# The prologue of a signature, attention and mixture-of-experts kernel: VectorE makes the first tile's levels, the norms come from Gram matrices

## The reference

```
x: 64 sequences x 64 steps x 7 channels; t is prepended: 8 channels
dx = x[:, 1:] - x[:, :-1]
levels 1 to 4 of the running path signature (8, 64, 512, 4096 values):
    e_k = outer(e_(k-1), dx) / k;  level_k += e_k + sum outer(level_i, e_(k-1-i))
h = concat(levels) @ W.T + b                                   # 4680 -> 128
h = h + attention(layernorm(h))    # 8 heads of 64, within a sequence, a token not to itself
h = h + moe(layernorm(h))          # 8 experts of 512, top 1, and a shared gelu expert

attention's weights are spectrally normed (one power iteration), for W = w_qkv and w_out:
    v = W @ u;  v = v / |v|;  u2 = W.T @ v;  u2 = u2 / |u2|
    sig = v @ W @ u2;  W / sig * sigma
```

## Time and profile before

| | |
|---|---|
| median of 3 runs | 715.73 us (715.45 to 715.82) |
| the profiled execution | 715.07 us, its span 713.1 us |
| TensorE busy over the span | 664.4 us, 93% |
| VectorE, GpSimd, ScalarE | 436.7, 334.1, 297.4 us |
| mean granted TensorE clock | 0.977 |
| prologue, up to TensorE's first product of iteration 0 | 54.10 us, TensorE busy 37.23 |
| iteration 0 | 14.33 us |

### The profile page before, as it was taken

How to read it: one execution, slowest core, us unless ns; L and a number is a source line. 1 busy time by engine, 2 the same in 40 slices (tenths; PEclk the granted TensorE clock), 3 DMA queues, 4 the chain that set the end, 5 groups by cost and what they waited for, 6 DMA issues and landing times.

```text
span 713.1 us, 13737 instructions
## 1 busy us (share of the span) xinstructions
PE 664.4 (93%) x3976; PEld 512.9 (72%) x3977; DVE 436.7 (61%) x1085; ACT 297.4 (42%) x701; POOL 334.1 (47%) x344
## 2 busy tenths in 40 slices
PE   4789999999999999999999999998879769999993
PEld 1567777777778777877777777876769737777772
DVE  6676776767766776767676776765374125445441
ACT  3314444454435444454435444443746124434440
POOL 5765453454435453455445443541027704544553
PEclk9799999999999999999999999999899979999998
DMA  8915221112211211112111211121244222323230
GB/s 329 171 64 203 49 47 33 37 34 61 63 37 33 58 37 37 33 44 52 33 37 33 63 33 37 33 56 41 66 173 136 75 56 40 42 39 41 38 41 5
DMA packets 40847, 45.28 MB, mean 63 GB/s; under 512 B 6272, under 2 KB 29184, under 8 KB 40448
## 3 DMA queue, kind: packets, MB, share of 16 engines
q1 hardware_dynamic: 34192, 40.86, 21.5%
q0 software_dynamic: 6640, 4.22, 4.3%
HBM read 17.30 MB, written 11.44 MB: 40 GB/s over the span
## 4 chain that ended last, share of the span: by engine, by line
PE 79%; POOL 8%; DVE 5%; issue 5%; DMA 1%; ACT 1%; SPq 0%; POOLq 0%; DVEq 0%
PE bank L1112 69%; POOL sorted_rows L523 4%; PE bank L1375 3%; PE bank L1271 2%; PE bank L1159 2%; PE bank L1251 1%; POOL e L432 1%; POOL e3l L444 1%; PE bank L1358 1%; POOL g L440 1%; POOL z L449 1%; DMA sq<-square 0%; PE bank L1193 0%; PE bank L1202 0%; DVE h L744 0%
## 5 line engine op out<-in xcount | busy, mean ns | idle before, releaser
L1112 PE MATMUL bank<-whigh,uth 128*128 128x512 f32 x512 | 168.4, 410 | 0.8 <-DVE lowt L740 0.8
L449 POOL TENSOR_TENSOR z<-z 128x512 f32<-128x512 f32 x32 | 40.8, 1276 | 182.3 <-DVE z L824 182.3
L1112 PEld LDWEIGHTS bank<-whigh,uth 128*128 128x128 f32 x512 | 89.8, 190 | 40.6 <-issue 25.5
L1112 PE MATMUL bank<-whigh,utl 128*128 128x512 f32 x256 | 100.9, 394 | 0.0
L531 POOL DMA_INDIRECT out<-z,ids x39 | 60.8, 1558 | 73.3 <-ACT z L703 73.0
L458 POOL TENSOR_TENSOR rstd<-rstd,powers 128x1 f32<-128x1 f32 x64 | 35.3, 552 | 71.3 <-DVE rstd L841 49.8
L1112 PE MATMUL bank<-xT,qkw 128*128 128x128 f32 x512 | 64.0, 279 | 0.0
L1085 DVE COPY xvp<-bank 128x512 f32<-128x512 f32 x39 | 27.0, 692 | 60.0 <-PE bank L1375 60.0
L562 ACT CAST uth<-bank 128x512 fp32r<-128x512 f32 x32 | 18.8, 586 | 105.6 <-PE bank L1164 105.6
L1112 PEld LDWEIGHTS bank<-xT,qkw 128*128 128x128 f32 x512 | 61.3, 196 | 0.1
L1112 PEld LDWEIGHTS bank<-whigh,utl 128*128 128x128 f32 x256 | 48.3, 189 | 11.2
(11 more groups left out here) (206 smaller groups left out, 1481.0 us busy)
## 6 DMA issues: line engine op xcount, KB each, us to landing
xvp<-xvo SPq DMA_DIRECT2D x128, 128.0 KB, 2.3
w<-w_t SPq DMA_DIRECT2D x1, 4096.0 KB, 13.4
sorted_rows<-x SPq DMA_DIRECT2D x3, 838.5 KB, 14.7
prob<-sorted_rows SPq DMA_DIRECT2D x39, 64.5 KB, 1.8
w<-w_high SPq DMA_DIRECT2D x4, 512.0 KB, 5.4
x_columns<-x2t SPq DMA_DIRECT2D x32, 64.0 KB, 1.6
xg_in<-x_columns SPq DMA_DIRECT2D x8, 256.0 KB, 3.2
levels<-w_t SPq DMA_DIRECT2D x1, 2048.0 KB, 8.6
```

Of the source, the lines that this page charges most:

```text
L449: G.tensor_tensor(z4[:], z[:, 0:4, :], z[:, 4:8, :], ALU.add).then_inc(tree, 1)
L1112: return T.matmul(out_, lhsT, rhs, start=start, stop=stop)
```

## The change

The reference, the loop and everything after it stay, with one exception named below.

- **Loads.** `before` is loaded by itself as third, `wqkv` fourth, then `ident`, then the other three matrices, then the signature weights, with the small arrays for the norms behind the first chunk. `wout` and the broadcast `u_out` are no longer loaded. A small array `u_columns` holds both u as columns.
- **Levels.** VectorE makes, in this order, `f2`, `e2` of group 0, `t3`, `low` of group 0, `t4`, `v3`, `g3` of group 0, adds the sum to `low`, makes `e3` of tile 0, adds to `g3`, makes `e3l` and `g4` of tile 0, and then `e2` of the other groups. GpSimd no longer does tile 0, and its `g3` products for the other groups come after `level3_rest(1)` and after all weight remainders.
- **Weight remainders** are all VectorE's.
- **Norms.** TensorE forms W.T W for `wqkv` (`gram_qkv`) and `wout` (`gram_wout`), VectorE multiplies the first by u and reduces, and TensorE multiplies the second by a column.
- **TensorE's order.** The query-key products come before `sum_level3(0)`, with the row halves alternating. Tile 0's projection does all high-part products of a half before the low-part ones. S2 of groups 1 to 3 moves behind.
- **In the loop**, GpSimd's `level3_rest(s)` waits for `xn_ready` of s-1 before `e3l`.

```
 sp.dma_start(xp_in, x_prev).then_inc(ld_x, 16)
-sp.dma_start(sq[:], square).then_inc(ld_sq, 16)
+sp.dma_start(sq[:, 1, :], square[:, 1, :]).then_inc(ld_before, 16)
+sp.dma_start(wqkv_sb, wqkv).then_inc(ld_w, 16)
+sp.dma_start(sq[:, 0, :], square[:, 0, :]).then_inc(ld_sq, 16)
+sp.dma_start(sq[:, 2:5, :], square[:, 2:5, :]).then_inc(ld_sq, 16)
 for c in range(UC):
     sp.dma_start(whigh_in[:, c, :], w_high[:, c, :]).then_inc(ld_sig[c], 16)
-sp.dma_start(wqkv_sb, wqkv).then_inc(ld_w, 16)
-sp.dma_start(woutT[:], wout_t).then_inc(ld_w, 16)
+    if c == 0:
+        sp.dma_start(uq[:], u_qkv).then_inc(ld_sn, 16)
+        sp.dma_start(ucol[:], u_columns).then_inc(ld_sn, 16)
+        sp.dma_start(scal[:], scalars).then_inc(ld_sn, 16)
+sp.dma_start(woutT[:], wout_t).then_inc(ld_wo, 16)
 sp.dma_start(wlow_in, w_low).then_inc(ld_sig[UC], 16)
-sp.dma_start(wout_sb, wout).then_inc(ld_sn, 16)
-sp.dma_start(uq[:], u_qkv).then_inc(ld_sn, 16)
-sp.dma_start(uo, u_out).then_inc(ld_sn, 16)
-sp.dma_start(scal[:], scalars).then_inc(ld_sn, 16)
...
@@ GpSimd @@
 def level3_rest(s, normed=True):
     pool.wait_ge(u4_sb, s)
     G.tensor_tensor(by3(g4), ...).then_inc(g4_ready, 1)
     pool.wait_ge(e3_hi, s + 1)
+    if normed:
+        pool.wait_ge(xn_ready, s - 1)
     G.tensor_tensor(e3l[:], e3[:], e3h[:].bitcast(F32), ALU.subtract).then_inc(e3_lo, 1)
...
+level3(1)
+level3_rest(1, False)
+pool.wait_ge(small, G3_INPUT_STEPS)
+pool.wait_ge(w_lo, UC + 1)
+rest = slice(512 // C2, TILES)
+G.tensor_tensor(g3[:, rest, :]..., spread(t4[:, rest, :], 3, shape), spread(v3[:, rest, :], 2, shape),
+                ALU.mult).then_inc(g3_outer, 1)
 add_channels(0)
 level3(2)
+root(0, ln1, 0)
 level3_rest(2)
-root(0, ln1, 0)
...
@@ ScalarE @@
 level3_hi(0)
+a.wait_ge(small, FIRST_LOW_STEPS)
 a.wait_ge(pads_zeroed, 1)
 low_features(0, True)
+for c in range(3):
+    signature_hi(c)
 features_hi(0)
+level3_hi(1)
+signature_hi(3)
...
 low_features(1)
 features_hi(1)
...
@@ VectorE @@
+d.wait_ge(s1_psum, 1)
+after(step(V.scalar_tensor_tensor(f2, v[:], 0.5, s1, ALU.mult, ALU.add)))
+level2(0)
+after(step(V.scalar_tensor_tensor(t3, v[:], 1.0 / 3.0, s1, ALU.mult, ALU.add)))
+low_outer(groups[0])
+step(V.scalar_tensor_tensor(t4, v[:], 0.25, s1, ALU.mult, ALU.add))
+made = step(V.tensor_scalar(v3, v[:], 1.0 / 3.0, None, ALU.mult))
+after(made)
+after(step(outer(g3[:, groups[0], :], t4[:, groups[0], :], v3[:, groups[0], :])))
+made = add_s2(0, first_level3)
+d.wait_ge(e3_hi, 1)
+V.tensor_tensor(e3l[:], e3[:], e3h[:].bitcast(F32), ALU.subtract).then_inc(e3_lo, 1)
+after(made)
+V.tensor_tensor(by3(g4), ...).then_inc(g4_ready, 1)
+level2(1)
+level4(0)
+level2(2)
+level2(3)
+signature_lo(0)
...
+features_lo(0)
+d.wait_ge(ld_sn, 48)
+d.wait_ge(norm_mm, 1)
+made = nstep(V.tensor_tensor(gram_u, B[5][:, 0:DIM], uq[:], ALU.mult))
+nstep(V.reduce_sum(wtwu[:], gram_u, axis=AX))
+for c in range(1, UC):
+    signature_lo(c)
+d.wait_ge(w_hi, UC + 1)
+remainder(wlow[lo_rows, 1, :], wlow_in[lo_rows, 1, :], wlow[lo_rows, 1, :], w_lo)
+level4(1)
...
+weigh(0, 0, True)
+weigh(0, 1)
+rest_made = low_outer(slice(per, TILES))
+features_lo(1)
+first_norm(0)
+first_norm_finish(0)
+after(rest_made)
+made = add_s2(1)
+d.wait_ge(norm_mm, 2)
+V.tensor_copy(gram_out, B[5][:, 0:DIM])
+made = nstep(V.tensor_copy(wu_out[:], B[5][:, DIM:DIM + 1]))
+V.tensor_tensor(nrm[:, 0:1], ucol[:, 0:1], wtwu[:], ALU.mult)
+V.tensor_tensor(nrm[:, 1:2], wtwu[:], wtwu[:], ALU.mult)
+V.tensor_tensor(nrm[:, 2:3], wu_out[:], wu_out[:], ALU.mult)
+add_s2(2)
+d.wait_ge(norm_mm, 3)
+made = nstep(V.tensor_tensor(nrm[:, 3:4], wu_out[:], B[5][:, DIM + 1:DIM + 2], ALU.mult))
+made = add_s2(3)
 level4(2)
+x_lo(0)
...
@@ TensorE @@
 def weight_products(banks, left, right):
-    for n in range(2):
-        for c in range(PAIRS):
+    for c in range(PAIRS):
+        for n in range(2):
...
+sum_level2(0)
+pe.wait_ge(ld_w, 16)
+weight_products(B[6:8], PAIRS, wqkv_sb[:, 0:PAIRS, :])
 pe.wait_ge(before_cast, 1)
 sum_level3(0)
 features(0, False)
+gram_qkv()
+project_first_hi(0)
 sum_level3(1)
+weight_products((B[5], B[4]), 2 * PAIRS, woutT)
+project_first_hi(1)
+sum_level2(1)
+sum_level2(2)
+project_first_lo(0)
+project_first_lo(1)
 features(1, False)
+pe.wait_ge(ww_lo, 2)
+sum_level2(3)
+gram_wout()
+project(1, 0, 1)
 accumulate(0)
+project(1, 1, UC + 1)
+mm(B[5][:, DIM + 1:DIM + 2], gram_out, wu_out[:]).then_inc(norm_mm, 1)
+x_columns(0)
 sum_level3(2)
+project(1, UC + 1, 9)
+mm(B[6][:, 256:260], ones, nrm[:]).then_inc(norm_mm, 1)
+project(1, 9, 10)
 features(2)
...
 iteration(0, True, True, True, False)
```

More of the change, by code:

```diff
@@ L80, in is_tile, with build @@
     return isinstance(i, int) and i == t
-def build(nc, x_next, x_prev, w_low, w_high, tok_b, wqkv, u_qkv, wout_t, wout, u_out, b_out,
+def build(nc, x_next, x_prev, w_low, w_high, tok_b, wqkv, u_qkv, wout_t, u_columns, b_out,
           scalars, gate_t, w13_t, w2_t, sw1_t, sw2_t, square, mask_c, steps, out):
@@ L541, in _, with signature_hi @@
             A = nc.scalar
-            a.wait_ge(ld_sq, 16)
-            A.copy(before_r[:], before).then_inc(before_cast, 1)
-            for c in range(UC):
+            def signature_hi(c):
                 a.wait_ge(ld_sig[c], 16)
@@ L762, in low_outer, with level2 @@
             def low_outer(ts):
                 return step(outer(low[:, ts, 1 + CHANNELS:LOW], t3[:, ts, :], vh[:, ts, :]))
-            after(f2_made)
-            for n, ts in enumerate(groups):
-                made = step(outer(e2[:, ts, :], f2[:, ts, :], v[:, ts, :]))
+            def level2(n):
+                made = step(outer(e2[:, groups[n], :], f2[:, groups[n], :], v[:, groups[n], :]))
                 assert made == E2_STEPS[n]
-                if n == 0:
-                    after(t3_made)
-                    first_made = low_outer(ts)
@@ L773, in add_s2 @@
-            def add_s2(n):
+            def add_s2(n, then=None):
                 s2 = B[SUM_BANKS[n]][:].rearrange("p (t c) -> p t c", c=C2)
                 d.wait_ge(s2_psum, n + 1)
-                step(V.tensor_tensor(low[:, groups[n], 1 + CHANNELS:LOW], low[:, groups[n], 1 + CHANNELS:LOW], s2,
-                                     ALU.add))
-                d.wait_ge(g3_outer, 1 if n == 0 else 2)
-                step(V.tensor_tensor(g3[:, groups[n], :], g3[:, groups[n], :], s2, ALU.add))
+                made = step(V.tensor_tensor(low[:, groups[n], 1 + CHANNELS:LOW],
+                                            low[:, groups[n], 1 + CHANNELS:LOW], s2, ALU.add))
+                if then:
+                    then(made)
+                if n:
+                    d.wait_ge(g3_outer, 1)
+                return step(V.tensor_tensor(g3[:, groups[n], :], g3[:, groups[n], :], s2, ALU.add))
@@ L1124, in _, with sum_level2 @@
             per = 512 // C2
-            for n in range(TILES // per):
+            def sum_level2(n):
                 pe.wait_ge(small, E2_STEPS[n])
```

236 lines of the change are left out of this document (102 added, 134 removed).

## The result

The changed kernel takes 706.18 us (median of 4 runs, 705.94 to 706.89) against 715.59 for the kernel before beside it (4 runs, 713.92 to 715.82): a ratio of 0.9875, 95% interval 0.9858 to 0.9892. The forecast was 706.5. The profiled execution took 706.33 us around a span of 704.5.

A forecast was written before the change was run, and what follows sets the result against it. TensorE fills the loop, so only iteration 0's start could move, held by one tile's latency: 54.1 to 45.0 us, 11.0 won before S3 of tile 0, 2 given back. That 9.1 gave 706.5 us, range 703.5 to 711.5.

The forecast's parts named there:

- Up to S3 of tile 0: Start of the prologue: VectorE alone makes tile 0's levels, `e3l` ready at 11.1 instead of 22.14 us; gain 11.0.
- gain of 1.4: First loads: `before` alone lands sooner, so the first product starts at 3.8 us, not 5.17; bounds 0 to 1.5.
- The alternating row halves: Query-key weight products before S3: alternating row groups takes the first set from 3.09 to 2.0 us, the second 1.1.
- TensorE's level: Gram products after tile 0's features: 5.1 us at 1.2 GHz, to 19.7; granted clock at 1.00 by about 20.
- The rival that it stays low until 31: Prologue: TensorE at 1.2 GHz until 31 us, iteration 0 at 50.2, 711.8 us; 0.19 together with VectorE's waits adding up.
- The two engines' work adds up: Prologue: VectorE and GpSimd slow each other when overlapping, so giving all to VectorE loses no parallel gain.
- a lump of 1.0: VectorE's constants after `u4` of tile 1: 1.0 us plus 1.0 added for GpSimd's held-back `g3` outer product beside them.
- The 1.3 put on VectorE: After weighing tile 0: VectorE's low outer product of the rest takes 1.74 us plus 1.3 beside `add_channels`.
- TensorE-bound: Prologue rival: VectorE slows less beside GpSimd and waits are short; iteration 0 at 41 to 43 us; chance 0.13.
- Slower by GpSimd's wait in the loop: Loop rival: the wait for `xn` makes `e3l` slow `prob`; from 0.8 us a turn slower than before; chance 0.04.
- No change: Rival: iteration 0 is held by ScalarE's wait for the fills or the big weight load; 715.7 us; chance 0.02.
- A loop still 14.3 an iteration: Loop: its instructions stay, so iterations keep 14.3 us with TensorE busy throughout; the wait for `xn` costs nothing.

The follow-up runs named there:

- E4: The changed kernel with the row halves of the weight products one after the other instead of alternating; ratio 0.9919 to the kernel before on the same chip.
- E12: E11 plus dummy products on TensorE before and around its first products, into a bank nothing reads then; ratio 0.9862 to the kernel before.
- E9: The changed kernel with the new 20-byte tile `ucol` allocated last instead of behind `woutT`; ratio 0.9874 to the kernel before.
- E7: E6 plus VectorE's low outer product of the other groups moved behind the low features of tile 1; ratio 0.9908 to the kernel before.
- E3: The changed kernel with `square` loaded whole, still as third load, instead of `before` by itself; ratio 0.9951 to the kernel before.
- E1: The changed kernel with GpSimd's `g3` products of the other groups no longer held back; ratio 0.9956 to the kernel before.
- E6: The changed kernel with VectorE's three constants (`ident_b`, `mask`, `tokbout`) made ahead of `wlow`'s remainder; ratio 0.9908 to the kernel before.
- E5: The changed kernel without GpSimd's wait for `xn` before `e3l` in the loop; ratio 0.9922 to the kernel before.
- E10: The kernel before with an unused tile of 20 bytes a partition allocated behind `woutT`; ratio 1.0014 to the kernel before.
- the control: The changed kernel itself, unedited, run again on chip B; 708.96 us, ratio 0.9925 to the kernel before there.
- E11: The changed kernel with the edits of E6 and E9 and two unused 32-byte tiles, ahead of `prob` and `xg_in`; ratio 0.9857 to the kernel before.

## Why the prediction was right, by its steps

**Up to S3 of tile 0: right as argued.** The first product came at 3.88 (said 3.8), `e3l` ended at 11.40 (11.1), S3 started at 11.55 (11.2), the features were transposed by 14.8 (14.6). The 0.3 are VectorE's products, 0.69 each when one stands alone instead of 0.63. S2 and the weight products stayed hidden; E4 and E12 made them 1.1 longer and 0.9 shorter and S3 did not move. Of the gain of 1.4 from loading `before` by itself the traces show between nothing (E9) and all of it (E11): that 3.8 was met was partly luck.

**The alternating row halves: right.** 1.95 and 1.16 against the 2.0 and 1.1 taken from a group that alternates between columns. Whether the row halves or the banks do it is not shown. The measured factor is 1.5 to 1.6, not the 2 that the Trainium skill's "TensorEngine Tiling (Array Packing)", section "Theoretical Speedup", gives as its most.

**TensorE's level: right in its outcome, and on the path as argued.** The Gram products took 3.90, not 5.1, since the level rose within them; the column was at 1.00 from 17 us. VectorE waited 0.68 us for them, where the forecast had 1.3. In the same program they took up to 4.80 in another execution (E7), and 5.08 in E4, so the 5.1 was within what happens. The rival that it stays low until 31 fell. It did fall again at 34, after an idle stretch of 1.40 us, which was in no step. The rival priced a low level up to 31 us at 5.2 us. In every trace it is over when the Gram products end (21.1 us at the latest, in E3; the next records take 0.40 us each), and what it costs there is 1.2 us at `x2n` from the best to the worst execution of one program. Before S3 it costs nothing (E12: S2 0.95 shorter, S3 no sooner), and from 34 to 37 us some 0.3: TensorE's `bank<-z,sq`, on the chain, takes 0.80 us in the changed kernel and 0.49 in E3 and E4, which have 25.66 behind `x2n` instead of 26.00.

**The two engines' overlaps: right that they cost, wrong in how.** "The two engines' work adds up" should read: an instruction of VectorE with both inputs in SBUF, or its cast or `tensor_scalar` from SBUF, and one of GpSimd's do not run side by side: the one that started later ends after the other, by its own length or less. E1 (13.08 against 12.52, 0.56 behind), E6 (2.73 to 0.22 for the same cast, which ended 0.08 behind) and E7 (0.46 to 2.07, 0.31 behind) show it in three places; `xn` with 1.09 us at 37.02 in the changed kernel, beside GpSimd's `g` at 36.97, is a fourth (0.07 behind). (This is the Trainium skill's "SBUF — State Buffer", section "SBUF: two separate sides": the shared port pair is an exclusive lock held for the whole instruction, and the other one fully blocks. The traces agree. By it the prediction would have had `ident_b` at up to 3.0 us, an estimate from the length of GpSimd's `g3`, instead of a lump of 1.0.) Where an operand came from a bank nothing was stretched, as I had it (0.67 to 0.69 us beside GpSimd in the changed kernel, E1 and E6). So the sum was right through errors that cancel. The three constants took 3.2 us (24.50 to 27.68) where 2.0 were allowed, and the Gram products ended at 18.5, not 19.7. The 1.3 put on VectorE for its low outer product beside `add_channels` did not come there (1.74, its usual length) but on GpSimd, whose add took 2.71 instead of 1.30. The low features ended at 33.0, not 35.0; the last chain, from there to iteration 0, took 11.6 us instead of 10.0, with that add, the lower level and 0.92 of idle time in it.

**The rivals.** "TensorE-bound" did not come, because of those overlaps; E6, which removes one, starts iteration 0 at 43.52. "Slower by GpSimd's wait in the loop" is refuted by E5. "No change" too: the load of 4 MB took 21.4 us from issue to landing, and no wait in the chain names it.

**"A loop still 14.3 an iteration": the step that failed.** 14.3 is iteration 0's length, and later ones took 14.5 in the kernel before already. Against that they grew by 0.07, and iteration 0 by 0.65. I had read the loop as unchanged because its instructions are; its operands' addresses are not, and E9 and E10 show that to be the whole of the 0.07, 1.9 us in all. It was covered by an iteration 30 and a tail that happened to be 1.8 us shorter. Of iteration 0's 0.65, 0.46 is TensorE's wait for GpSimd's adds at 49.12, behind VectorE's `weigh(1, 1)`, which the norm's last steps precede. About 0.1 goes with the address: E9's iteration 0 takes 14.87 and the control's 14.95, E10's 14.42 and that of the kernel before 14.33. The rest was not separated.

**How firm is the hit?** In the runs of the result the ratio was 0.9875, on chip B 0.9925, with intervals that don't meet. The mechanism is the same in both traces; 706.5 against 706.18 is partly luck, and a gain of 5 to 9 us is what the runs support. The shorter prologue, 8.9 to 9.5 us by the traces, does not come through whole on chip B. The traces of the changed kernel, 704.5 and 705.8 us of span, differ by 1.3: 0.6 by TensorE's level at S3 and in the Gram products, 1.1 by iteration 30 (13.80 against 12.64), less 0.3 behind it. The kernel before was 1.3 faster on chip B (714.29 against 715.59). That leaves 1.5 of the 4.1 us between the two gains. The control's traced run was the fastest of its six (707.66, median 708.96), and no trace of the kernel before from that chip was there to say more.

## What to carry to other kernels

Where a prologue is one tile's latency, count the chain in the order of need, and put it on one engine; what helps is less the engine than that nothing is done ahead of need. Place each of GpSimd's instructions beside those of VectorE that read a bank, and work that reads SBUF where GpSimd waits: one small cast in the wrong place took 2.5 us more, and 1.1 at iteration 0. When a new small tile is added, put it behind the hot ones; E11 does so, pads two other places, and has the lowest ratio, 0.9857, though E9's and E12's intervals overlap it. And before a difference of 1 us between two traces is put down to an edit, look whether it is there ahead of the edit: at `x2n` one program differed from itself by 1.2.

## What the runs showed of the hardware that was not expected

- **An address costs time on TensorE.** 32 bytes beside a multiple of 64 made an iteration 14.58 us instead of 14.51. Which operand does it was not separated. The 512 records of `whigh,uth` take 409 to 412 ns on average in the four traces with most tiles at multiples of 64 (before, E9, E11, E12) and 413 to 415 in the ten others.
- **The level did not follow idle time alone.** It fell after 1.40 us idle in the changed kernel; in E7 it stayed at 1.00 across an idle 1.07 at 34 us. In E12 it was up at 6.58 us and down again at 14. In E6 S3's first record took 0.47 us and in E7 0.76, with the same program up to there, and the same pair stands in the changed kernel and its control. No run here separates what decided.
- **Chips differ.** The same kernel before took 714 to 716 us in the runs of the result and on chip B, and 735 to 737 on chips A and C, 3% more, though on C its prologue is as long as before (54.16 in E10). The difference lies behind the loop: from the start of iteration 31 to the end it is 209.8 to 211.5 us in all six traces of the result and of chip B, and 230.9 to 233.4 in all eight of chips A and C. Where in it: from 530 to 560 us TensorE was busy for 28.69 us in the changed kernel's profile of the result and for 10.63 in E9 on chip C, GpSimd for 22.83 and 22.81 in both.
